# A gated low-rank FFN on one core: the 128x128 turn of the gated rows as 32x32 blocks on VectorE, with a new order of the low-rank work and of the first products

## The reference

```python
y = einsum('bct,bcd->bdt', x, weights[condition])         # mix of the 64 rows of a group
result = y @ W_base.T + b_base                             # 1024 x 1024
probs  = softmax(y @ W_gate.T)                             # 8 experts
top_p, top_i = top_k(probs, 2); top_p /= sum(top_p)
hw     = (y @ A.T) * route_w                               # 8 x 16 = 128 gated columns
out    = x + result + hw @ B
```

## Time and profile before

| what | us |
|---|---|
| median of 3 runs (lowest to highest) | 947.48 (947.12 to 949.1) |
| the profiled execution | 946.93 |
| its span, first to last instruction | 945.2 |
| TensorE busy | 938.7 (99%) |
| VectorE busy | 427.7 (45%) |
| ScalarE busy | 380.2 (40%) |
| POOL busy | 535.5 (57%) |

### The profile page before, as it was taken

How to read it: one execution, slowest core, us unless ns; L and a number is a source line. 1 busy time by engine, 2 the same in 40 slices (tenths; PEclk the granted TensorE clock), 3 DMA queues, 4 the chain that set the end, 5 groups by cost and what they waited for, 6 DMA issues and landing times.

```text
span 945.2 us, 16847 instructions
## 1 busy us (share of the span) xinstructions
PE 938.7 (99%) x5474; PEld 882.7 (93%) x5474; DVE 427.7 (45%) x1328; ACT 380.2 (40%) x810; POOL 535.5 (57%) x506
## 2 busy tenths in 40 slices
PE   8999999999999999999999999999999999999998
PEld 7999999999999999999999999999999999999997
DVE  5784344443444433444434444344444344443444
ACT  6463343434334333334334343333443343434332
POOL 3575547655566555575555665455655546655560
PEclk9999999999999999999999999999999999999999
DMA  9522332233322233332333222333223332233312
GB/s 303 188 79 101 133 113 98 89 111 122 133 89 94 95 122 133 111 96 92 108 125 128 94 86 103 122 133 107 89 88 115 133 112 99 89 111 122 133 49 86
DMA packets 41453, 107.15 MB, mean 113 GB/s; under 512 B 4449, under 2 KB 8674, under 8 KB 41442
## 3 DMA queue, kind: packets, MB, share of 16 engines
q1 hardware_dynamic: 41440, 107.01, 32.9%
q10 hardware_dynamic: 2, 0.00, 0.0%
HBM read 73.43 MB, written 33.55 MB: 113 GB/s over the span
## 4 chain that ended last, share of the span: by engine, by line
PE 97%; DVE 1%; DMA 1%; ACT 0%; SPq 0%; issue 0%; DVEq 0%
PE ps L787 54%; PE ps_r L787 19%; PE ps_out L805 11%; PE ps_out L815 9%; PE ps L846 3%; PE ps_hwt L811 1%; DMA w_sum<-in_w_t 1%; DVE w_sum L603 1%; PE ps_r L846 1%; DVE o_sb L633 0%; PE ps L832 0%; PE ps_r L832 0%; ACT a_hi L413 0%; DVE w_lo L596 0%; ACT w_hi L425 0%
## 5 line engine op out<-in xcount | busy, mean ns | idle before, releaser
L311 POOL TENSOR_TENSOR a_lo<-raw,a_hi 128x512 fp32r<-128x512 f32 x128 | 166.1, 1317 | 247.7 <-ACT a_hi L413 247.7
L620 DVE TENSOR_TENSOR z_sum<-ps,z_sum 128x448 f32<-128x448 f32 x150 | 93.7, 624 | 241.1 <-PE ps L787 241.1
L787 PE MATMUL ps<-w_hi,s_hi 128*128 128x448 f32 x480 | 177.6, 370 | 0.0
L787 PE MATMUL ps<-w_lo,s_hi 128*128 128x448 f32 x480 | 175.5, 366 | 0.0
L787 PE MATMUL ps<-w_hi,s_lo 128*128 128x448 f32 x480 | 173.6, 362 | 0.0
L787 PE MATMUL ps_r<-r_lo,a_hi 128*128 128x264 f32 x496 | 140.9, 284 | 0.0
L787 PE MATMUL ps_r<-r_hi,a_hi 128*128 128x264 f32 x496 | 140.6, 284 | 0.0
L787 PE MATMUL ps_r<-r_hi,a_lo 128*128 128x264 f32 x496 | 140.5, 283 | 0.0
L787 PE MATMUL ps<-w_hi,a_hi 128*128 128x448 f32 x360 | 134.0, 372 | 0.0
L787 PE MATMUL ps<-w_lo,a_hi 128*128 128x448 f32 x360 | 131.1, 364 | 0.0
L633 DVE TENSOR_TENSOR o_sb<-ps_out,o_sb 128x448 f32<-128x448 f32 (+1 forms) x192 | 94.3, 506 | 80.9 <-PE ps_out L815 80.7
(11 more groups left out here) (96 smaller groups left out, 1629.8 us busy)
## 6 DMA issues: line engine op xcount, KB each, us to landing
raw<-in_x_t SPq DMA_DIRECT2D x128, 256.0 KB, 2.8
o_sb<-in_x SPq DMA_DIRECT2D x64, 512.0 KB, 3.9
out_x<-o_sb SPq DMA_DIRECT2D x62, 512.0 KB, 2.6
w_sum<-in_w_t SPq DMA_DIRECT2D x8, 448.0 KB, 9.2
r_raw<-in_w_t SPq DMA_DIRECT2D x4, 264.0 KB, 5.5
table_raw<-in_cond_w SPq DMA_DIRECT2D x2, 256.0 KB, 8.8
b_raw<-in_b_t SPq DMA_DIRECT2D x1, 512.0 KB, 11.0
out_x<-o_sb SPq DMA_DIRECT2D x2, 224.0 KB, 2.2
```

The source lines that it names most:

```text
L311: pool.tensor_tensor(a_lo[j][:], raw[j][:], as_f32(a_hi[j][:]), ALU.subtract).then_inc(s_a_lo[j], 1)
L620: return dve.tensor_tensor(to, bank[:, 0:NS], other, ALU.add)
L787: mm = pe.matmul(bank[:, 0:w.shape[-1]], a[:, k, :], w[:, k, :], start=(opens and k == 0 and q == 0), stop=(closes and k == KH - 1 and q = ...
```

## The change

Tiles 3 to 61 are no longer turned by TensorE: VectorE turns `hw` in 16 blocks of 32x32 into `hwt_sum`, which shares its memory with `hwt_lo`. `hwt_top` waits for 16 blocks of each tile and reads `hwt_sum`; `hwt_rest` reads `hwt_sum` too. Tiles 0, 1, 2, 62 and 63 keep the turn on TensorE (`pe_hwt_top`). POOL makes the rest of S4 before the mix table of b:

```diff
 hwt_hi = sb("hwt_hi", [P, P], F32R)
-hwt_lo = sb("hwt_lo", [P, P], F32R)
+hwt_sum, hwt_lo = shared("hwt_sum", "hwt_lo", [P, P])
...
         a_rest(p, A22)
         pool.wait_ge(s_mixed[0][Q], p)
         fetch_mix(p, 0)
+        s_rest(p, 4, raw[A12][:], s2_hi, s2_lo)
         pool.wait_ge(s_mixed[1][R], p)
         fetch_mix(p, 1)
-        s_rest(p, 4, raw[A12][:], s2_hi, s2_lo)
         if not last:
             prepare(p + 1)
...
     def hwt_top(i):
-        act.wait_ge(s_hwt, i + 1)
+        act.wait_ge(s_turned, BLOCKS * (i - 2))
+        act.copy(hwt_hi[:], hwt_sum[:]).then_inc(s_hwt_hi, 1)
+
+    def pe_hwt_top(n):
+        act.wait_ge(s_hwt, n)
         act.copy(hwt_hi[:], ps_hwt[:, 0:P]).then_inc(s_hwt_hi, 1)
```

ScalarE's step, with a function of its own for the last pair:

```diff
-        exps(3)
         a_top(2, A21)
...
         act.wait_ge(s_p[1], p + 1)
+        act.wait_ge(s_mixed[1][L], p)
         act.copy(z_sum[1][:, cols(L)], ps_1[:, 0:NS]).then_inc(s_p1_out, 1)
-        hwt_top(2 * p - 1)
+        exps(2 * p - 1)
         act.wait_ge(s_p[6], p + 1)
         sum_top(p, 4, raw[A12][:], s2_hi)
+        hwt_top(2 * p - 1)
         act.wait_ge(s_p[2], p + 1)
         z_top(0, L, ps_1[:, 0:NS])
-        seed(p, 0, L)
         act.wait_ge(s_r_sum[0], p + 1)
         z_top(0, R, ps_r[:, 0:width[R]])
+        if not last:
+            a_top(p + 1, A11)
+        seed(p, 0, L)
+        if not last:
+            a_top(p + 1, A12)
         seed(p, 0, R)
         seed(p, 0, Q)
-        if not last:
-            a_top(p + 1, A11)
         exps(2 * p)
-        if not last:
-            a_top(p + 1, A12)
-            sum_top(p + 1, 3, s3[:], s3_hi)
+        if last:
+            finish(p)
+            return
+        sum_top(p + 1, 3, s3[:], s3_hi)
         added_top(p, 1, Q)
-        if not last:
-            sum_top(p + 1, 1, s1[:], s1_hi)
+        sum_top(p + 1, 1, s1[:], s1_hi)
         added_top(p, 1, L)
         hwt_top(2 * p)
         added_top(p, 0, Q)
-        seed(p, 1, L)
-        if last:
-            seed(p, 1, R)
-            exps(2 * p + 1)
-            seed(p, 1, Q)
-            return
         sum_top(p + 1, 2, s2[:], s2_hi)
-        exps(2 * p + 1)
         act.wait_ge(s_r_sum[1], p + 1)
         z_top(1, R, ps_r[:, 0:width[R]])
+        a_top(p + 1, A21)
+        a_top(p + 1, A22)
+        seed(p, 1, L)
         seed(p, 1, R)
         seed(p, 1, Q)
-        a_top(p + 1, A21)
-        a_top(p + 1, A22)
+
+    def finish(p):
+        act.wait_ge(s_z_lo[0][L], p + 1)
+        act.copy(ps_1[:, 0:NS], bias[:, cols(Q)]).then_inc(s_seed[Q], 1)
+        added_top(p, 1, Q)
+        added_top(p, 1, L)
+        act.copy(ps_6[:, 0:NS], bias[:, cols(L)]).then_inc(s_seed[L], 1)
+        pe_hwt_top(4)
+        added_top(p, 0, Q)
+        exps(2 * p + 1)
+        seed(p, 1, R)
+        pe_hwt_top(5)
+        act.wait_ge(s_r_sum[1], p + 1)
+        z_top(1, R, ps_r[:, 0:width[R]])
     pairs(act, first, step)
-    hwt_top(TILES - 1)
-    act.wait_ge(s_r_sum[1], PAIRS)
-    z_top(1, R, ps_r[:, 0:width[R]])
```

VectorE ranks and weighs b at the beginning of the next step; a's blocks stand four at a time between its other work:

```diff
     u2 = z_sum[0][:, cols(Q)]
     u3 = z_sum[1][:, cols(Q)]
-    def hwt_rest(i):
+    def turn_hw(i, parts=range(P // TURN)):
+        dve.wait_ge(s_hw, i + 1)
+        for c in parts:
+            for r in range(P // TURN):
+                dve.transpose(hwt_sum[c * TURN:(c + 1) * TURN, r * TURN:(r + 1) * TURN],
+                              hw[r * TURN:(r + 1) * TURN, c * TURN:(c + 1) * TURN]).then_inc(s_turned, 1)
+
+    def hwt_rest(i, whole=ps_hwt[:, 0:P]):
         dve.wait_ge(s_hwt_hi, i + 1)
-        dve.tensor_tensor(hwt_lo[:], ps_hwt[:, 0:P], as_f32(hwt_hi[:]), ALU.subtract).then_inc(s_hwt_lo, 1)
-
-    def output(p, t, c):
+        dve.tensor_tensor(hwt_lo[:], whole, as_f32(hwt_hi[:]), ALU.subtract).then_inc(s_hwt_lo, 1)
+
+    def output(p, t, c, bank=None):
...
         t_rest(4, NT4)
         z_rest(1, 1, L, ps_1[:, 0:NS])
         z_rest(1, 1, R, ps_r[:, 0:width[R]])
-        rank_experts(1, 1)
-        weigh_experts(1, 1)
     def step(p, last):
+        rank_experts(p - 1, 1)
+        weigh_experts(p - 1, 1)
+        turn_hw(2 * p - 1)
         dve.wait_ge(s_p1_out, p - 1)
         dve.wait_ge(s_p[6], p + 1)
         add(ps_6, p1, u2).then_inc(s_u2, 1)
-        hwt_rest(2 * p - 1)
+        hwt_rest(2 * p - 1, hwt_sum[:])
+        z_rest(p, 0, L, ps_1[:, 0:NS])
+        z_rest(p, 0, R, ps_r[:, 0:width[R]])
         output(p - 1, 1, L)
-        z_rest(p, 0, L, ps_1[:, 0:NS])
         output(p - 1, 1, Q)
         output(p - 1, 1, R)
-        z_rest(p, 0, R, ps_r[:, 0:width[R]])
-        rank_experts(p, 0)
         dve.wait_ge(s_p[7], p + 1)
         add(ps_6, p1, u3).then_inc(s_u3, 1)
+        rank_experts(p, 0)
         weigh_experts(p, 0)
+        if not last:
+            turn_hw(2 * p, (0,))
         dve.wait_ge(s_p[5], p + 1)
         dve.wait_ge(s_u3, p - 1)
         add(ps_5, u3, u3).then_inc(s_z_sum[1, Q], 1)
+        if not last:
+            turn_hw(2 * p, (1,))
         added_rest(p, 1, Q)
+        if not last:
+            turn_hw(2 * p, (2,))
         dve.wait_ge(s_p[4], p + 1)
         add(ps_6, p1, p1).then_inc(s_z_sum[1, L], 1)
+        if not last:
+            turn_hw(2 * p, (3,))
         added_rest(p, 1, L)
-        hwt_rest(2 * p)
+        if not last:
+            hwt_rest(2 * p, hwt_sum[:])
         dve.wait_ge(s_p[3], p + 1)
         dve.wait_ge(s_u2, p - 1)
         add(ps_5, u2, u2).then_inc(s_z_sum[0, Q], 1)
+        if last:
+            finish(p)
+            return
+        added_rest(p, 0, Q)
+        z_rest(p, 1, R, ps_r[:, 0:width[R]])
         output(p, 0, L)
+        output(p, 0, R)
+        output(p, 0, Q)
+
+    def finish(p):
+        hwt_rest(2 * p)
         added_rest(p, 0, Q)
+        rank_experts(p, 1, ps_6)
+        weigh_experts(p, 1)
+        output(p, 0, L)
         output(p, 0, R)
-        rank_experts(p, 1)
-        if last:
-            weigh_experts(p, 1)
-            output(p, 0, Q)
-            return
+        hwt_rest(2 * p + 1)
+        output(p, 0, Q)
         z_rest(p, 1, R, ps_r[:, 0:width[R]])
-        output(p, 0, Q)
-        weigh_experts(p, 1)
+        output(p, 1, L, ps_6)
+        output(p, 1, Q, ps_1)
+        output(p, 1, R)
     pairs(dve, first, step)
-    hwt_rest(TILES - 1)
-    z_rest(PAIRS - 1, 1, R, ps_r[:, 0:width[R]])
-    for c in (L, Q, R):
-        output(PAIRS - 1, 1, c)
```

TensorE's prologue makes the first two pieces of R and B11 by kinds, each kind behind its own wait:

```diff
-    for piece in range(2):
-        first_r(ps_r, 0, piece)
-        first_r(ps_5, 1, piece)
-    first_q(ps_1, 0, 0, "B11").then_inc(s_p[1], 1)
-    first_q(ps_6, 1, 0, "B11").then_inc(s_p[6], 1)
+    HH, HL, LH = range(3)
+
+    def first_kind(bank, t, j, kind, u_hi, u_lo, n):
+
+        u, v = ((a_hi, u_hi), (a_hi, u_lo), (a_lo, u_hi))[kind]
+        for k in range(2 * j, 2 * j + 2):
+            mm = pe.matmul(bank[:, 0:n], u[2 * t][:, k, :], v[:, k, :], start=(k == 0 and kind == HH),
+                           stop=False)
+        return mm
+
+    def r_kind(t, j, kind):
+        return first_kind((ps_r, ps_5)[t], t, j, kind, r_hi, r_lo, width[R])
+
+    def b11_kind(t, j, kind):
+        return first_kind((ps_1, ps_6)[t], t, j, kind, w_hi[:, B11], w_lo[:, B11], NS)
+
+    pe.wait_ge(s_a_hi[A11], 1)
+    pe.wait_ge(s_r_hi, 1)
+    r_kind(0, 0, HH)
+    pe.wait_ge(s_a_lo[A11], 1)
+    r_kind(0, 0, LH)
+    pe.wait_ge(s_r_lo, 1)
+    r_kind(0, 0, HL)
+    pe.wait_ge(s_a_hi[A21], 1)
+    r_kind(1, 0, HH)
+    r_kind(1, 0, HL)
+    pe.wait_ge(s_r_hi, 2)
+    r_kind(0, 1, HH)
+    r_kind(0, 1, LH)
+    r_kind(1, 1, HH)
+    pe.wait_ge(s_a_lo[A21], 1)
+    r_kind(1, 0, LH)
+    r_kind(1, 1, LH)
+    pe.wait_ge(s_r_lo, 2)
+    r_kind(0, 1, HL)
+    r_kind(1, 1, HL)
+    for j in range(2):
+        pe.wait_ge(s_w0_hi["B11"], j + 1)
+        for t in range(2):
+            b11_kind(t, j, HH)
+            b11_kind(t, j, LH)
+        pe.wait_ge(s_w0_lo["B11"], j + 1)
+        for t in range(2):
+            mm = b11_kind(t, j, HL)
+            if j == 1:
+                mm.then_inc(s_p[(1, 6)[t]], 1)
     first_r(ps_r, 0, 2)
```

In a step of TensorE the mix L of b follows P1 of the next pair, b's low rank follows R of a, and a's mix Q and low rank end the pair. In the last pair b's L and Q go to `ps_6` and `ps_1` (`mix_chunk`, `lora`, `output` and `rank_experts` have got a bank for it):

```diff
         pe.wait_ge(s_z_lo[0][R], 2)
         plain_r(ps_r, 1, 0, True, False)
         plain_r(ps_r, 1, 1, False, True).then_inc(s_r_sum[1], 1)
-        mix_chunk(1, 1, L)
+        pe.wait_ge(s_z_lo[1][L], 2)
         for t in (1, 2, 3, 4):
...
         strassen(ps_1, a_hi[A11], a_lo[A11], B11, True).then_inc(s_p[1], 1)
+        mix_chunk(p - 1, 1, L)
+        pe.wait_ge(s_s_lo[2], p - 1)
+        strassen(ps_6, s2_hi, s2_lo, T2, True).then_inc(s_p[6], 1)
         mix_chunk(p - 1, 1, Q)
         mix_chunk(p - 1, 1, R)
-        pe.wait_ge(s_s_lo[2], p - 1)
-        strassen(ps_6, s2_hi, s2_lo, T2, True).then_inc(s_p[6], 1)
-        turn_hw(2 * p - 1)
         pe.wait_ge(s_p1_out, p - 1)
         pe.wait_ge(s_a_lo[A12], p + 1)
         strassen(ps_1, a_hi[A12], a_lo[A12], B21, False).then_inc(s_p[2], 1)
+        plain_r(ps_r, 0, 0, True, False)
+        plain_r(ps_r, 0, 1, False, True).then_inc(s_r_sum[0], 1)
         pe.wait_ge(s_hwt_lo, 2 * p)
...
         lora(1, R)
-        plain_r(ps_r, 0, 0, True, False)
```

(60 more changed lines are left out.)

## The result

| | before | after |
|---|---|---|
| median, us (lowest to highest) | 947.99 (947.12 to 949.1, 4 runs) | 1023.34 (1021.59 to 1023.91, 4 runs) |
| span of the profiled execution | 945.2 | 1021.9 |
| mean granted clock of TensorE | 1.000 | 0.986 |

The ratio after to before is 1.0789, 95% interval 1.0773 to 1.0805: 8% slower, where 0.8% faster was forecast.

The account below looks back on a forecast made before the run. TensorE's instruction stream was taken to bound the kernel (busy 938.7 of 945.2 us). Terms of -6.4 (turns), -0.4 (head) and -0.45 (tail) summed to -7.2 us, giving 940.1 us, range 938.8 to 943.5.

Parts of the forecast that it names:

- Part 1: Loop on TensorE: 59 of 64 tile transposes, 0.108 us each, move to VectorE, so 6.4 us go.
- Part 2: VectorE's turns: 16 block transposes of 32x32 per tile at 0.10 us each, 1.6 us per tile (1.3 to 5.6).
- rival A: VectorE becomes late in the loop: TensorE stalls from 0.25 us per block; at 0.35, 984 us; chance 6%.
- Part 3: Loop over pairs of tiles: VectorE's added work and the other new waits are all hidden, at a cost of 0.
- 4.2 of room: b's turn: VectorE's low part ends at 7.6 us of the pair, the low rank wants it at 11.76.
- the room of 0.8: a's turn: z(a,Q) complete at 25.93 us, wanted by its mix at 26.75; the least room in the pair.
- rival B: VectorE and POOL collide in the loop: up to 0.3 us stall, 0.05 to 0.2 on average, 943 us; chance 14%.
- Part 4: The kernel's two ends: 0.4 us less at the start, 0.45 us less at the finish.
- The head: Kernel's start: R and B11 1.07 us earlier, of which 0.4 us is left after the seed wait (bounds 0 and 1.1).
- The tail: Kernel's end: TensorE's idle wait for seed(b,Q) goes, 0.1 us of stall is new; 0.45 us less.

Follow-up runs that it names:

- the order alone: Changed kernel with all 64 turns back on TensorE, its new order, first products by kinds and end kept: 948.05 us against 948.07 for the kernel before, ratio 1.0001.
- POOL held back: Changed kernel plus two POOL waits, S3's low part for z_lo of b's Q and S2 for a's hwt_lo: 942.34 us, ratio 0.9943 to the kernel before.

## Why the prediction was wrong

*Part 1, what leaves TensorE.* Right but for 0.05: with the turns away and no collision, the pair is 28.83 us against 28.99 before (28.78 forecast). The 0.05 are R's longer steps, which the kernel with the order alone has too, and the wait of 0.04; over 29 pairs they are 1.5 of the 7.2 us forecast. The sum put the new order at nothing.

*Part 2, what a block costs.* This term of the sum was mis-sized: 0.10 was taken, 0.23 measured. I set a block between two of the ranking's small operations, whose steps are 0.09 and 0.14, and gave the number of elements the say. But here no block starts before the one ahead is done: 0.20 of duration plus 0.03. A tile costs 3.7 us and not 1.6. The argument against rival A, that every small operation starts within 0.15 of the one before, was a wrong reading besides: behind the `top` at 501.31 the same time line has a step of 0.20.

```profile
501.51 0.23 DVE L644 COPY h_sb<-ps_out 128x64 f32<-128x64 f32 x1
```

*Part 3, whether it is hidden.* This is the step that failed, and it failed in its second half. The time table was right: b's blocks are hidden (4.2 of room), rival A's threshold of 0.25 per block held (at 0.23 and nothing else there is 0.04 of wait), and the room of 0.8 before the mix of a's Q was 0.7. What failed was the price of rival B. I gave POOL and VectorE one collision of at most 0.3 in effect, from the earlier trace rows, and treated it as apart from the price of a block. They are one thing: with the blocks VectorE begins `z_lo` of b's Q 3.1 before R of b, with the turns on TensorE 3.9, and this 0.8 is enough to stand behind S3's low part, which in the order of before went after it; the 0.60 lost there carries it into S2, and the 0.75 lost there carries it into S4, where `hwt_lo`, newly with two SBUF inputs, takes 1.37 in place of 0.28. 2.44 us of collision came on top of blocks that had used up the room, and 2.37 of them are in the pair. Neither A nor B at the price I gave it could reach 1023; I had set their chances at 6% and 14% and had no case of both.

The Trainium skill's page SBUF — State Buffer, section SBUF: two separate sides, has the rule that fits: an exclusive lock between the two engines, held for the whole instruction. The traces agree: the three subtractions end 0.48, 0.49 and 0.15 after POOL's operation, no more than the 0.62, 0.62 and 0.28 that they take alone, so they wait for its end and are not slowed beside it; and with one input in PSUM `hwt_lo` does not wait (0.278).

*The clock.* No step named it. 12.5 of the 76.7 us are dips after the hole.

*Part 4, the ends.* The head gained nothing that the medians show, where 0.4 was forecast. TensorE starts R early (5.63), but in the execution after the seed let the first mix go at 28.59, later than the 28.02 of the earlier trace rows, because the bias landed about 0.9 later; between executions that landing moves by more than the step was worth. I had seen the limit, not its spread. The tail went nearly as laid out, by the chains of the kernels with the order alone and with POOL held back: no wait at b's last mix Q and 0.15 to 0.20 at a's. From the start of the last P4 to the end of TensorE's work are 13.20 and 13.22 us in them, 13.57 before, so about 0.35 of the 0.45 came.

*What would have told.* The time lines of VectorE and POOL in the kernel before have it:

```profile
494.24 0.66 DVE L613 TENSOR_TENSOR z_lo<-z_sum,z_hi 128x448 fp32r<-128x448 f32 x1 [0.63 <-ACT z_hi L432]
...
494.38 1.67 POOL L315 TENSOR_TENSOR s_lo<-s_sum,s_hi 128x512 fp32r<-128x512 f32 x1
```

POOL's low part of S3 took 1.67, where 1.29 is its time alone: it waited, as VectorE was first by 0.14. A change that makes VectorE later by more than that, with POOL where it was, turns the order round, and then VectorE, which is on the path, is the one that waits.

## What to carry to other kernels

Where two engines exclude each other, the order in which they arrive is part of the schedule: before putting work on an engine with spare time, look in each stage which of the two comes second now, and by how little. A busy share of 45% says nothing of that, and many small instructions cost more by their number than by their elements. If a new lateness does flip the order, holding back the engine that has room can be enough: two waits on POOL brought 1023.34 us to 942.34. A quarter of the instructions on VectorE gave 941.25, but with the turn left incomplete.

## What was not expected of the hardware

- VectorE's 32x32 fp32 transpose: 0.203 us each, 0.234 apart when each signals, 0.213 when none does, 0.223 long and 0.254 apart into PSUM; 32x128 in one instruction 0.303. They do not overlap, while a copy of 0.22 (501.17 in the earlier trace rows) has the next operation 0.14 behind it. Each block reads or writes another quarter of the partitions than the one ahead, which the copy does not, and no run tells whether this or the transposing keeps the blocks apart.
- After waits of 1.8 and 2.1 us in every pair TensorE's clock fell to 1.2 GHz in 3 and in 8 of the pairs, for 3.4 us (steps of 0.375 in place of 0.202); each time 1.56 us were lost.
- The landing of one and the same bias transfer moved the first seed between 26.3 and 28.3 us over twelve profiled executions.
